# Top-k attention decoder layer on one core: temperature summed on VectorE, three biases off TensorE, engines reordered, a sixteenth candidate admitted

## What is computed

```python
q, k, v = heads(x @ Wq + bq), heads(x @ Wk + bk), heads(x @ Wv + bv)   # 16 heads of 32
qn, kn = q / norm(q), k / norm(k)
temp = sigmoid(x.mean(axis=1) @ Wt + bt) + 0.5                          # one number per batch
scores = (qn @ kn.T) / temp
vals, idx = top_k(scores, 256 // 4)                                     # keep 64 of 256 per row
w = softmax(vals)                                                       # scattered back, zeros elsewhere
out = (w @ v) @ Wo + bo
gate = sigmoid(x @ Wg + bg)
x1 = layernorm(x + gate * out + (1 - gate) * x)
x2 = layernorm(x1 + softmax((x1 @ xWq + xbq) @ (ctx @ xWk + xbk).T) @ (ctx @ xWv + xbv))
x3 = layernorm(x2 + sum_k w_k * (x2 @ W[ids_k].T + b[ids_k]))           # eight adapters, fused into one
```

## Time and profile before

| | before |
|---|---|
| time, median of 3 runs | 3458.11 us (3455.98 to 3460.54) |
| profiled execution, its own time | 3452.61 us |
| its span, first to last instruction | 3450.8 us |
| mean granted TensorE clock | 0.935 |
| busy: PE, DVE | 2917.6 us, 2918.5 us (85% each) |
| busy: ACT, POOL | 2135.9 us (62%), 1669.9 us (48%) |
| `cross_max`, once per batch | 32 times, at 213.5 to 3407.5 us |

### The profile page before, as it was taken

How to read it: one execution, slowest core, us unless ns; L and a number is a source line. 1 busy time by engine, 2 the same in 40 slices (tenths; PEclk the granted TensorE clock), 3 DMA queues, 4 the chain that set the end, 5 groups by cost and what they waited for, 6 DMA issues and landing times. The chain is left out here.

```text
span 3450.8 us, 60452 instructions
## 1 busy us (share of the span) xinstructions
PE 2917.6 (85%) x16154; PEld 1602.4 (46%) x16154; DVE 2918.5 (85%) x10240; ACT 2135.9 (62%) x5970; POOL 1669.9 (48%) x2285
## 2 busy tenths in 40 slices
PE   6799989988988789888988899799978889889845
PEld 3454555544544344444444544455544444445423
DVE  3888989889888888888898898888988899888982
ACT  2676767666666556665665676566756666566641
POOL 4355545545544355344544455455534555445523
PEclk9899999999999899999999999899989999989977
DMA  6000000000000000000000000000000000000000
GB/s 210 7 17 23 23 23 20 23 5 23 23 23 20 4 23 23 22 20 5 23 23 23 23 20 21 7 23 23 23 20 4 23 23 23 23 20 17 4 16 13
DMA packets 43577, 80.46 MB, mean 23 GB/s; under 512 B 3787, under 2 KB 11979, under 8 KB 43059
## 3 DMA queue, kind: packets, MB, share of 16 engines
q1 hardware_dynamic: 41554, 69.18, 6.0%
q0 software_dynamic: 1504, 5.77, 0.5%
HBM read 58.16 MB, written 16.78 MB: 22 GB/s over the span
## 5 line engine op out<-in xcount | busy, mean ns | idle before, releaser
L517 POOL TENSOR_SCALAR probs<-probs,kept_inv 128x256 f32<-128x256 f32 x1024 | 486.9, 496 | 921.5 <-DVE kept_inv L1770 921.5
L1732 DVE SCALAR_TENSOR_TENSOR probs<-scores,threshold,probs 128x256 f32<-128x256 f32 x1006 | 440.2, 502 | 110.8 <-ACT probs L782 54.9
L807 ACT ACTIVATE probsT<-work_ps 128x512 f32<-128x512 f32 x512 | 291.4, 597 | 290.9 <-PE work_ps L1029 253.5
L1684 DVE TENSOR_SCALAR near<-scores,flip 128x256 int32<-128x256 int32 x1024 | 468.4, 526 | 3.4
L772 ACT ACTIVATE scores<-score_ps,neg_guess 128x256 f32<-128x256 f32 x1024 | 397.4, 484 | 99.4 <-DVE kept_inv L1770 90.2
L1029 PE MATMUL work_ps<-ident,probs 128*128 128x128 f32 x2072 | 325.9, 295 | 152.1 <-POOL probs L517 94.0
L792 ACT ACTIVATE near<-scores 128x256 f32<-128x256 f32 x1024 | 414.1, 423 | 21.6 <-DVE nearest L1700 19.8
L1696 DVE MATCH_REPLACE8 near<-nearest,near 128x256 f32<-128x256 f32 x1024 | 407.6, 411 | 0.0
L1692 DVE MAX8 nearest<-near 128x8 f32<-128x256 f32 x1024 | 358.6, 412 | 6.4 <-DVE near L1684 4.7
L1700 DVE MAX8 nearest<-near 128x8 f32<-128x256 f32 x1024 | 358.1, 414 | 0.0
L484 POOL TENSOR_TENSOR inv_norm<-sumsq,minus_half 128x32 f32<-128x32 f32 x64 | 351.4, 5491 | 5.3
(11 more groups left out here) (171 smaller groups left out, 5523.9 us busy)
## 6 DMA issues: line engine op xcount, KB each, us to landing
x_in<-in_x_dram SPq DMA_DIRECT2D x32, 512.0 KB, 4.0
x_res<-in_x_dram SPq DMA_DIRECT2D x32, 512.0 KB, 4.6
out_dram<-rows SPq DMA_DIRECT2D x32, 512.0 KB, 3.1
c_sb<-in_ctx_dram SPq DMA_DIRECT2D x32, 256.0 KB, 2.7
scores<-in_L_ffn_W_dram SPq DMA_DIRECT2D x6, 1024.0 KB, 5.8
near<-in_L_ffn_W_dram SPq DMA_DIRECT2D x2, 1024.0 KB, 9.8
w_q<-in_L_attn_Wq_dram POOLq DMA_DIRECT2D x1, 1024.0 KB, 9.1
w_k<-in_L_attn_Wk_dram POOLq DMA_DIRECT2D x1, 1024.0 KB, 11.0
```

The costliest lines, as they stand in the source:

```text
L517: pool.tensor_scalar(probs[:, s % 2, h, j], probs[:, s % 2, h, j], kept_inv[:, s % 2, n:n + 1], 1.0, ALU.mult, ALU.mult).then_inc(s_pr, 1)
L807: act.activation(probsT[:, h, 2 * a:2 * a + 2], W[BANK_TP[s][2 * h + a]][:].rearrange("p (h k n) -> p h k n", h=2, k=NT), ACT.Copy).then_i ...
L1684: last = dve.tensor_scalar(near[:, h, j].bitcast(I32), scores[:, r, h, j].bitcast(I32), flip[:, r, n:n + 1].bitcast(I32), None, ALU.bitwis ...
L1732: step.mark(dve.scalar_tensor_tensor(out=probs[:, r, h, j], in0=scores[:, r, h, j], scalar=threshold[:, r, k:k + 1], in1=probs[:, r, h, j] ...
```

## The change

What it does:

- **Temperature.** `sum_x` on DVE sums `xT` over the tokens (one reduction 128x1024 to 128x4) and multiplies by the weights; `temp` on PE is one matmul 128x4 with ones; `take_temp` reads 4 columns in place of 256.
- **Biases.** Query, key, gate and output projections keep the fifth matmul. The value bias goes through `w_o` into the output bias once; the cross value bias and the adapter bias are added by POOL to `x1` and `x2` for the whole batch (`bias_x1`, `bias_x2`, 128x1024 each).
- **Sixteenth.** The last rank becomes a real one. `set_threshold` counts a row as unsure if its sign sum is `LAST_BELOW` (-160) or if equal neighbours exist.
- **Orders.** All bodies are rewritten, with other PSUM banks; the front of batch 0 is written out ahead of the bodies, with the fusing work spread in it. The adapters are loaded in two halves to other buffers, and `load_x(1)` stands between them.

The core of the diff:

```diff
+        LAST_BELOW = float(2 * (KEEP - WINDOW) - S)
-                    last = pool.memset(ranks[:, n:n + 1], (2.0 * n + 1.0) ** 2 - MIDDLE ** 2 if n < WINDOW - 1 else 0.5)
+                    last = pool.memset(ranks[:, n:n + 1], (2.0 * n + 1.0) ** 2 - MIDDLE ** 2)
...
-                dve.tensor_scalar(unsure[:, r], n_same[:], 1.0, None, ALU.not_equal).then_inc(s_bad, 1)
+                dve.scalar_tensor_tensor(out=unsure[:, r], in0=sign_sum[:, r], scalar=LAST_BELOW, in1=n_same[:],
+                                         op0=ALU.not_equal, op1=ALU.not_equal).then_inc(s_bad, 1)
...
+            def sum_x(b):
...
+                step.wait(step.mark(dve.tensor_reduce(x_sums[:, 0], xT[:], AX.X, ALU.add)))
+                dve.tensor_tensor(x_sums[:, 1], x_sums[:, 0], wt_cols[:], ALU.mult).then_inc(s_xw, 1)
...
-                    mm = pe.matmul(W[BANK_TMP][:, 0:S], wt_wide[:, kt], xT[:, kt], start=kt == 0, stop=kt == KD - 1)
+                pe.wait_ge(s_xw, at(b, 1, 1))
+                pe.matmul(W[BANK_TMP][:, 0:KD], ones[:], x_sums[:, 1], start=True, stop=True).then_inc(s_tmp_f, 1)
...
-                project(W[BANK_V[t]][:], xT, w_v, BV, t).then_inc(s_v_f, 1)
+                project(W[BANK_V[t]][:], xT, w_v, None, t).then_inc(s_v_f, 1)
-                project(W[BANK_XV[t]][:], pcT, w_vx, BVX, t, KC).then_inc(s_xv_f, 1)
+                project(W[BANK_XV[t]][:], pcT, w_vx, None, t, KC).then_inc(s_xv_f, 1)
-                project(W[BANK_F[t]][:], x2T, w_f, BF, t).then_inc(s_f_f, 1)
+                project(W[BANK_F[t]][:], x2T, w_f, None, t).then_inc(s_f_f, 1)
...
+            def bias_x1(b):
+                pool.wait_ge(s_x1t_f, at(b, NT, NT))
+                pool.tensor_tensor(x1, x1, cross_bias_wide[:].unsqueeze(1).to_broadcast([P, NT, D]), ALU.add)\
+                    .then_inc(s_x1b, 1)
...
+            sum_x(0)
+            key_sums(0, 0)
+            temperature(0)
+            query_sums(0, 0)
+            query_sums(0, 1)
+            widen_value_bias()
+            adapter_shares()
+            adapters(0, 1)
+            key_sums(0, 1)
+            adapters(1, 2)
+            adapters(2, 3)
+            split_late_biases()
+            adapters(3, 4)
+            query_moments(0, 0)
+            query_moments(0, 1)
+            moments(0)
+            after_guesses()
+            adapters(4, 5)
+            adapters(5, 6)
+            adapters(6, 7)
+            adapters(7, 8)
```

More of the change, by code:

```diff
@@ L565, in body @@
                 if behind:
+                    scale_probs(i - 1, 2, 1)
+                if here:
+                    if where != "first":
+                        guesses(i)
+                if behind:
+                    scale_probs(i - 1, 3, 0)
+                    scale_probs(i - 1, 3, 1)
+                    out_minus_x(i - 1, 0, 1 - p)
+                    out_minus_x(i - 1, 1, 1 - p)
                     norm1(i - 1, 1 - p)
@@ L568, in body @@
                     scale_probs(i, 0, 0)
+                if behind:
+                    bias_x1(i - 1)
+                if here:
                     scale_probs(i, 0, 1)
                 if ahead:
-                    norms(i + 1, 0)
+                    if where != "fill":
+                        norms(i + 1, 0)
                 if behind:
@@ L925, in body @@
-                if behind:
                     take_probs(i - 1, 3, 0, 0)
@@ L956, in body @@
                     take_x1(i - 1, 1)
+                if here:
+                    exps(i, 1, 0)
+                    exps(i, 1, 1)
+                if ahead:
+                    if where != "fill":
+                        take_query(i + 1, 0)
+                if behind:
                     take_ctx(i - 1)
@@ L962, in body @@
                     take_cross_scores(i - 1)
-                if here:
-                    copy_scores(i, 2, 1)
+                if ahead:
+                    if where != "fill":
+                        take_temp(i + 1)
                 if behind:
@@ L1107, in project @@
                 for kt in range(kts):
-                    pe.matmul(dst, src[:, kt, t * P:t * P + P], w[:, kt], start=kt == 0, stop=False)
+                    mm = pe.matmul(dst, src[:, kt, t * P:t * P + P], w[:, kt], start=kt == 0,
+                                   stop=bias is None and kt == kts - 1)
+                if bias is None:
+                    return mm
+                if first:
+                    pe.wait_ge(s_bias, 1)
                 return add_bias(dst, bias)
@@ new lines, in body @@
+                    if where != "fill":
+                        if where == "first":
+                            pe.wait_ge(s_v, at(i, 2, 2))
+                        else:
+                            pe.wait_ge(s_pt, at(i - 1, 16, 16))
+                        key(i + 1, 0)
+                    if where != "fill":
+                        if where == "first":
+                            pe.wait_ge(s_empty, 15)
+                        else:
+                            pe.wait_ge(s_at, at(i - 1, 4, 4))
+                        query(i + 1, 0)
@@ L1464, in body @@
                     turn_cross(i - 1)
[L1465 to L1472 removed]
+                    if where in ("last", "drain"):
+                        pe.wait_ge(s_x1t, at(i - 1, 2, 2))
+                    else:
+                        pe.wait_ge(s_tmp, at(i + 1, 1, 1))
@@ new lines, in body @@
+                if ahead:
+                    if where != "fill":
+                        if where == "first":
+                            pe.wait_ge(s_kc, at(i + 1, 2, 1))
+                        else:
+                            pe.wait_ge(s_xv, at(i - 1, 2, 2))
+                        key(i + 1, 1)
+                if here:
+                    pe.wait_ge(s_fl, at(i, 4, 2))
+                    turn_probs(i, 0, 1, 1)
+                if ahead:
+                    if where != "fill":
+                        pe.wait_ge(s_pt, at(i, 16, 2))
+                        gate(i + 1, 0)
```

1035 lines of the change are left out of this document (561 added, 474 removed).

## The result

The changed kernel takes 3492.31 us (median of 4 runs, 3482.78 to 3495.64), the kernel before beside it 3458.01 (4 runs). The ratio is 1.0094, 95% interval 1.0073 to 1.0115: slower by 0.9%, where 5.4% faster was forecast. The profiled execution took 3493.35 us with a span of 3491.2 and a mean granted clock of 0.914 (before 0.935).

A forecast was written before the change was run, and what follows sets the result against it. The prediction took PE and DVE handing work to each other as the bound, DVE's 86 us the floor. 3450.8 - 58 - 105 (3.5 per period, 30 periods) - 23 - 1.5 = 3263.3 us of span, said as 3270; range 3165 to 3370.

The forecast's parts named there:

- Struck heads, -58: Heads on the slow path: 18 become 13 with the sixteenth usable, saving 58 us in all.
- PE, -4.1 per period: Six bias matmuls and the wide temperature product leave PE; its relief reaches each period one for one, -4.1 us.
- Rival (b): Whole kernel: DVE is the bound and PE's relief is worth nothing, a period +0.6 us, 3393 us; chance 0.06.
- DVE, +1.4: The token sum and its short product on DVE add 1.4 us per period, with nothing to hide them.
- POOL, +0.6: POOL's two bias sums, 3.9 us, cost a period 0.6 us by meeting DVE's turns, spread evenly.
- Rival (c): POOL's sums block DVE fully, +3.3 us per period on the forecast, 3369 us; chance 0.04.
- Order, -1.4: The new instruction orders in a period shorten DVE's waits for the exponential and the signs, less lost cover: -1.4 us.
- rival (e): `keep_top(i, 0)` waits for the count with less cover, DVE idle 8 us per period, 3510 us; chance 0.04.
- Front, -23: Before the first mark: earlier key product, norms and guesses bring batch 0's sides forward, less some lost again: -23 us.
- End, -1.5: The last chain through cross attention and adapters loses four bias matmuls: -1.5 us.

The follow-up runs named there:

- b_pe: b_six without the bias matmuls of value, cross value and adapters on PE, nothing put in their place: 3399.77 us.
- b_dve: b_six with the token sum of x and its product added on DVE, ahead of the turns of step 1, result unread: 3394.39 us.
- b_pool: b_six with POOL's two 128x1024 sums added to x1 and x2 (adding temperature weights), PE's bias matmuls kept: 3445.01 us.
- a_nobias: The changed kernel without POOL's two sums on x1 and x2, biases of cross value and adapters left out: 3368.51 us.
- a_turn: The changed kernel with both turns of step 1 put back ahead of the masks of step 0 on DVE: 3325.95 us.
- b_all2: The kernel before with all the changed work in the old order, `sum_x` ahead of the turns of step 1 on DVE: 3487.48 us.
- b_six: The kernel before with one edit, the sixteenth neighbour made usable: 3397.83 us.

## Why the prediction was wrong, step by step

- **Struck heads, -58**: right (-57.8).
- **PE, -4.1 per period, "taken at one for one"**: the step that failed first. b_pe measures 0 for 2.3 of the 4.1; the temperature's 1.8 were not measured by themselves. The argument compared two periods of before, of 93.9 us at a clock of 1.00 and of 97.4 at 0.96, and took the slow clock as the cause of the longer period. A wait comes first there too. The period of 97.4 us (second below) has a wait of 2.8 us that the one of 93.9 (first) lacks; "issue" names no other engine for it. It ends at 638.80 us, and right behind it PE runs at 0.50 for 6.6 us. Rival (b), given 0.06, is right in what it says of PE. The longest of PE's waits from 307.8 to 401.7 us, then from 596.0 to 693.4 us, and the stretch behind the latter:

```profile
PE work_ps L1217 <- DVE unsure L1719: 1.7, 1, 1.7
```

```profile
PE work_ps L1029 <- issue: 2.8, 1, 2.8
```

```profile
638.80:645.40 6.60, 6.22 (x31) 4.67 (x32) 5.98 (x29) 4.06 (x11) 2.37 (x6) 0.50 0.01 5
```

- **DVE, +1.4**: the work was a little more, 1.22 for the sum and 0.47 for the product, which had been put at 0.17. Its cost is 0: less idle time before the masks makes up for it, in b_dve together with shorter turns. "Nothing hides it, since DVE is the fuller engine" was wrong.
- **POOL, +0.6**: in the order of before 46.6 us in 31 periods, +1.5 (b_pool); in the changed one 118.5, +3.8 (a_nobias). One sum takes 2.35 to 2.39 us, not 1.96. "Spread evenly" was wrong: `kept_inv` starts DVE's next instructions and POOL's scaling in the same moment, so the turns behind it meet POOL in every batch. Rival (c), with 0.04, has nearly this price, 3.9 in all, but in part by luck: it let both sums block DVE, while 109 of the 118 us come from the sum on x1, by the chain above.
- **Order, -1.4**: what I missed is what the moved turns now stand beside. Put back, they give 161 us, 5.2 per period (a_turn). This and POOL's 3.8 price the same meeting from two sides, so they are not to be added. Other parts came as forecast: the wait for the exponential is gone, that for the signs is smaller (92.9 us in all, 107.3 before), and the turns even take less in all, 396.4 us for 468.4; a sum over the run hides the one place that matters. The cover taken from `keep_top(i, 0)` is a wait of 1.5 us at a time, of the kind that rival (e) has, though not of 8. Its 3510 is the number on record nearest to 3492, and that is luck.
- **Front, -23**: 17. The turns of batch 0 begin at 70.9 us and not at 100.3, close to the 72.4 worked out for the choice of sides; what then takes 12 of those 29 back before the first mark exceeds the 4.5 that I had put down for it. The working also takes 12.3 us off the end of the second `normalise` where it has 10.8 off its first norm, and gives no reason for the 1.5. **End, -1.5**: -1.1.

The instances of the turns (ns min, median, max, first and last start) in the kernel before, and of the turns and MAX8 in the changed one:

```profile
L1684 DVE TENSOR_SCALAR near<-scores,flip x1024: 300/350/2000, 100.3 to 3356.0; 128x256 int32<-128x256 int32 x171
```

```profile
L1844 DVE TENSOR_SCALAR near<-scores,flip x1024: 301/348/2442, 70.9 to 3396.7; 128x256 int32<-128x256 int32 x171
L1852 DVE MAX8 nearest<-near x1024: 398/408/429, 73.0 to 3408.5; 128x8 f32<-128x256 f32 x171
```

Even the good order is 56 us above the forecast of 3270: two plain periods of a_turn, as they stand below, take 95.7 and 95.2 us, 1.2 to 1.7 less than the 96.9 of before, where 3.5 were forecast.

```profile
1890.90:1986.60 95.70, 83.98 (x492) 46.16 (x491) 85.65 (x307) 66.42 (x189) 56.69 (x75) 0.98 0.06 21
2177.70:2272.90 95.20, 83.86 (x491) 46.78 (x490) 85.42 (x306) 66.13 (x187) 54.13 (x70) 0.98 0.07 22
```

Three things stay open. b_all2 is 88 us over b_six, while its parts measured apart (b_pe, b_dve, b_pool) sum to 44. In its trace PE waits 88.5 us for ACT's copy of the adapters' product (b_six 1.7, b_pe 34.1), and a matmul of `cross_left` takes 439 ns for 385; whether this comes from the temperature that PE, ACT and DVE now pass between them, from `cross_left` ahead of `turn_ctx`, or from the parts acting together, no run tells. Why less work on DVE made a_turn slower is not settled. And how much of the chain's price is PE's wait and how much its clock was not measured apart.

## What to carry to other kernels

Before work is taken off an engine to save time, leave it out and measure: here 72 us less of PE's busy time were worth nothing, although PE was the busiest engine beside DVE. When an instruction is moved behind one that releases another engine, look at what that engine starts in the same moment, and whether the two can run together; here one swap of neighbours on DVE was worth 161 us, and the struck heads, the front and the end together 76. Where a period is long and its clock low, look for a wait ahead of the low stretch before pricing work at the low clock: in both places looked at here there was one.
